# Score halves, then the k and q projections, then the k and q transposes: a new order on TensorE in a windowed-attention pipeline

## The reference, cut to what matters

```
for l in range(2):
    h = shift_token(x)                         # second half of the channels from the token before
    q, k, v = split(h @ wqkv[l], 3)            # 8 heads of 64 channels
    q = l2norm(q) * q_scale[l]; k = l2norm(k) * k_scale[l]
    q, k = rotary_xpos(q, k)                   # a*cos*scale + rotate_half(a)*sin*scale
    o = local_attention(q, k, v)               # windows of 128: own window and the one before, softmax
    x = x + o @ wo[l]
    h = layernorm(shift_token(x)) * ln_g + ln_b
    a, g = split(h @ w1[l] + b1[l], 2)
    x = x + (a * gelu(g)) @ w2[l] + b2[l]
```

## Time and profile before

| | |
|---|---|
| three timed runs | 3395.86, 3398.49, 3399.98 us, median 3398.49 |
| the profiled execution, own time | 3400.02 us |
| its span | 3398.2 us, mean granted TensorE clock 0.956 |
| busy in the span | PE 91%, weight loads 85%, VectorE 74%, ScalarE 70%, GpSimd 54% |
| chain that ended last | PE 77%, VectorE 13%, issue 6% |
| stage 1 | until about 655 us |
| stage 2, steps 4 to 12 (pipeline fills) | 690 to 850 us |
| layer 0 | to about 1978 us; a pair of an even and an odd step takes 42.57 us |
| layer 1 | to about 3290 us; a pair takes 40.92 us |

### The profile page before, as it was taken

The page is one execution under the profiler, slowest core; times in us unless marked ns, Lnnn a source line. Parts: engine busy times, 40 slices in busy tenths (PEclk is TensorE's granted clock), DMA queues, the critical chain, the costliest instruction groups (busy, mean ns, idle before and its releaser), DMA issues.

```text
span 3398.2 us, 68852 instructions
## 1 busy us (share of the span) xinstructions
PE 3089.9 (91%) x22436; PEld 2901.1 (85%) x22436; DVE 2507.5 (74%) x7244; ACT 2394.6 (70%) x5499; POOL 1848.1 (54%) x1761
## 2 busy tenths in 40 slices
PE   7776664179999999999999999999999999999998
PEld 6665553168999999999999989999999999999998
DVE  5999999768777777777777757666667666676664
ACT  4756566457777777777777767777777777777774
POOL 3666666545555555555555545555555555555543
PEclk9988887589999999999999999999999999999999
DMA  2131100155444444444444445544444444444441
GB/s 82 39 136 42 51 27 19 50 117 129 110 109 111 106 111 113 105 107 111 107 111 110 101 125 119 154 110 104 103 103 107 113 111 106 106 106 111 111 102 32
DMA packets 262521, 333.65 MB, mean 98 GB/s; under 512 B 40978, under 2 KB 159508, under 8 KB 261140
## 3 DMA queue, kind: packets, MB, share of 16 engines
q1 hardware_dynamic: 262164, 329.25, 39.4%
HBM read 77.33 MB, written 42.05 MB: 35 GB/s over the span
## 4 chain that ended last, share of the span: by engine, by line
PE 77%; DVE 13%; issue 6%; SPq 1%; DMA 1%; ACT 1%; POOL 1%; DVEq 0%; POOLq 0%; ACTq 0%
PE ps L408 42%; PE ps L490 12%; PE ps L476 6%; PE ps L464 4%; PE ps L465 4%; PE ps L451 3%; DVE aS L891 2%; PE ps L385 2%; PE ps L499 2%; DVE num L899 1%; DVE q L906 1%; DVE BS L927 1%; DVE mS L940 1%; DVE f L916 1%; SPq L1555 1%
## 5 line engine op out<-in xcount | busy, mean ns | idle before, releaser
L751 ACT ACTIVATE Sm<-Sm,nb,sc 128x256 f32<-128x256 f32 (+1 forms) x1024 | 597.6, 588 | 0.8
L1100 DVE CUSTOM_DVE_ANT_0 Sm<-ps,mask 128x256 f32<-128x256 f32 (+1 forms) x1024 | 369.2, 417 | 170.6 <-PE ps L465 168.6
L490 PE MATMUL ps<-vv,PT 128*128 128x64 f32 x4032 | 478.4, 272 | 0.0
L490 PEld LDWEIGHTS ps<-vv,PT 128*128 128x128 f32 x4032 | 470.4, 192 | 0.0
L1173 DVE SCALAR_TENSOR_TENSOR Gl<-ps,vecs,Gl 128x256 f32<-128x256 f32 (+1 forms) x384 | 173.4, 479 | 329.6 <-PE ps L408 284.4
L408 PE MATMUL ps<-zTh,W1h 128*128 128x256 f32 (+1 forms) x1408 | 409.2, 291 | 0.0
L729 ACT ACTIVATE sq<-ps 128x512 f32<-128x512 f32 x256 | 153.2, 599 | 348.2 <-PE ps L408 348.2
L408 PE MATMUL ps<-zTl,W1h 128*128 128x256 f32 (+1 forms) x1408 | 397.2, 282 | 0.0
L408 PE MATMUL ps<-zTh,W1l 128*128 128x256 f32 (+1 forms) x1408 | 391.7, 278 | 0.0
L1380 POOL TENSOR_TENSOR uTl<-Gl,uTh 128x512 fp32r<-128x512 f32 (+1 forms) x192 | 212.9, 1109 | 321.5 <-ACT uTh L800 185.0
L1246 POOL TENSOR_TENSOR rs<-rs,mhalf 128x16 f32<-128x16 f32 x128 | 372.5, 2910 | 0.0
(11 more groups left out here) (189 smaller groups left out, 9538.1 us busy)
## 6 DMA issues: line engine op xcount, KB each, us to landing
kkh<-kh SPq DMA_DIRECT2D x512, 128.0 KB, 2.4
kkl<-kl SPq DMA_DIRECT2D x512, 128.0 KB, 2.4
qq<-qTh SPq DMA_DIRECT2D x256, 128.0 KB, 2.4
qq<-qTl SPq DMA_DIRECT2D x256, 128.0 KB, 2.4
tb<-tab SPq DMA_DIRECT2D x128, 128.0 KB, 2.5
xc<-x SPq DMA_DIRECT2D x32, 256.0 KB, 2.9
rwkv_scratch<-rw SPq DMA_DIRECT2D x32, 256.0 KB, 2.1
rk<-rwkv_scratch SPq DMA_DIRECT2D x64, 128.0 KB, 2.5
```

Source lines behind the costliest of these rows:

```text
L490: ins = pe.matmul(PS[:, k, 64 * i:64 * i + 64], PT[:, h, s * 128:(s + 1) * 128], vv[:, v, h, :], start=s == sides[0], stop=s == sides[-1])
L751: act.activation(Sm[:, h, c0:c1_], Sm[:, h, c0:c1_], ACT.Exp, bias=nb[:, h:h + 1], scale=sc[:, n % 4, h:h + 1], accum_out=sm[:, n % 2, h:h ...
L1100: dve.tensor_tensor_reduce(Sm[:, h, c0:c1_], PS[:, bank["scores", n, q, h % 2], (h // 2 % 2) * 256 + c0:(h // 2 % 2) * 256 + c1_], mask[:, ...
```

## The change

The order inside a step changes in two places that must agree: the list of PSUM users, and TensorE's loop. No instruction is added or removed, and no other engine's program is edited. Waits and increments stay the same, except for the waits on read-outs, which follow from the ring.

```diff
@@ psum_order2
     if live(4):
         yield "scores", t - 4, 0, 0
         yield "scores", t - 4, 0, 1
+        yield "scores", t - 4, 1, 0
+        yield "scores", t - 4, 1, 1
     if live(2):
         yield "qkv", t - 2, 1
-    if live(4):
-        yield "scores", t - 4, 1, 0
-        yield "scores", t - 4, 1, 1
+        yield "qkv", t - 2, 0
     if live(3):
         yield "qkT", t - 3, 1
-    if live(2):
-        yield "qkv", t - 2, 0
-    if live(3):
         yield "qkT", t - 3, 0
     if live(2):
         yield "qkv", t - 2, 2
@@ tensor_program, the loop over t
                 if live(4):
                     scores(t - 4, 0)
+                    scores(t - 4, 1)
                 if live(2):
                     qkv(t - 2, 1)
-                if live(4):
-                    scores(t - 4, 1)
+                    qkv(t - 2, 0)
                 if live(3):
                     turn_qk(t - 3, 1)
-                if live(2):
-                    qkv(t - 2, 0)
-                if live(3):
                     turn_qk(t - 3, 0)
                 if live(2):
                     qkv(t - 2, 2)
```

## The result

The changed kernel takes 3420.22 us (median of 4 runs, 3418.15 to 3421.36), the kernel before 3398.93 on the same chip: a ratio of 1.0063, 95% interval 1.0046 to 1.0081. It is slower by 21 us, on the side that was forecast, but by nearly twice the 11.7 of the sum, and above the range of 3401 to 3417.

The account below looks back on a forecast made before the run. TensorE's own time was taken to bound the kernel, with x2_out on VectorE also pacing layer 0. Terms +6.5 + 3.0 + 3.1 - 0.9 + 0 = +11.7 gave 3411.7, as median 3410; range 3401 to 3417 us.

Parts of the forecast that it names:

- the sum: All terms added for the whole kernel: +11.7 us against the profiled execution's 3400.0, so 3411.7.
- Direction: Whole kernel: slower by over 0.2%, above 3405.3 us, chance 0.72.
- the three waits: ScalarE's queue in layer 0, VectorE's wait in the fill, a bank wait in layer 1: +6.5, +3.0, +3.1 us.
- (c): Pipeline fill: VectorE's rotation of k waits for the later transposes of k, 0.38 late in eight steps, +3.0 us.
- (d): Layer 1, behind odd steps: turn_z waits for its bank until the later q rotation ends, 0.10 a pair, +3.1 us.
- (a): TensorE, eight transposes in a row: saves between nothing and 10 us, taken as 0.
- (b): Odd steps of layer 0: ScalarE's late square of k delays v_out through x2_out, W2 waits 0.25 longer, +6.5 us.
- (e): Border of the layers: 0.95 us of scores now run before the wait for WQ's reload, -0.9 us.
- Rival 4: Slower by more: second bank wait in layer 1's even steps, upper ends of (b) and (c); +19, 3417, chance 0.11.
- Rivals 1 and 2: No measurable change, 3402, chance 0.20; or faster, one return from transposes to products less, 3390.5, chance 0.06.
- Rival 3: TensorE: grouped transposes drop the clock, the v part runs at 1.2 GHz, +164 us, 3574, chance 0.01.

Follow-up runs that it names:

- act_first: Changed kernel with ScalarE's last high part of u and pre_norm moved ahead of the square of k: 3406.67 us, ratio 1.0023.
- two_ak: Changed kernel with two buffers for the rotated k, so its rotation waits for older transposes: 3412.82 us, ratio 1.0046.
- other_bank: Changed kernel with only the bank list reordered, transposes of k ahead of the q part, TensorE's order untouched: 3413.28 us, ratio 1.0038.
- two_ak_act_bank: Changed kernel with the edits of act_first, other_bank and two_ak together: 3392.18 us, ratio 0.9979.
- half_act: half_scores plus the ScalarE edit of act_first: 3389.04 us, ratio 0.9971 against the kernel before.
- half_scores: Kernel before with only scores 1 moved ahead of the k part, transposes left in place: 3405.99 us, ratio 1.0019.
- group_turns: Kernel before with only the q part moved ahead of the transposes of k, scores still split: 3410.00 us, ratio 1.0028.
- tail_late: Changed kernel with VectorE's subtraction of the tail of u moved from ahead of k's rotation to behind the sums: 3429.66 us, ratio 1.0089.

## Why the prediction was wrong, point by point

- **Direction, and the three waits**: right. All three waits that were named are in the profile after, and each goes when its cause is taken away (act_first, two_ak, other_bank). What was missing is under (c) and (d).
- **(a) grouping the transposes, 0**: right within its bounds; two_ak_act_bank against half_act measures a gain of 1.6 us. In layer 0 the eight transposes start at 1164.55 and the v part's first two products at 1165.34 and 1165.65: 0.31 between these, as said, and 1.10 - 0.23 = 0.87 for the eight.
- **(b) ScalarE's queue, +6.5**: right: +5.6 in layer 0 by the table, 0.22 per pair over 25 pairs (0.24 by the medians). half_scores has it alone, act_first takes it away.
- **(c) VectorE's wait in the fill, +3.0**: right in kind, too small in size: +5.1, and just above the upper bound of 5. The distance of 0.81 was exact, but two_ak shows that without the wait the fill would have been 2.5 us shorter than before: the wait costs 7.6. half_scores, with 2.0 less in the fill, points to the earlier scores for the gain. So the 3.0 owes part of its nearness to luck: it left out a gain and a larger cost that stand against each other. Why each step loses as much as it does was not traced further.
- **(d) the ring in layer 1, +3.1: this is the step that failed.** 28 pairs lost 10.6 us, 0.38 a pair (0.36 by the medians) instead of 0.10. The 0.10 of the late rotation is there (group_turns). The distance of turn_z behind the read-out was taken from W2, which starts 0.05 behind; turn_z starts 0.15 behind: another 0.10 a pair. And "VectorE works through from there" left out what stands ahead of the rotation in its queue: ScalarE's delay of (b) was followed to v_out in layer 0 and not to u_hi's other reader, the subtraction of the tail. It meets GpSimd's low part, takes 0.32 longer, and so the rotation of k is 0.25 late instead of 0.10 (20.69 us behind the first product with WO, 20.44 before). That is worth 0.17 a pair by half_scores, the same by other_bank against act_bank (41.07 and 40.90), and 0.15 by act_first against the changed kernel (41.13 and 41.28).
- **(e) the border, -0.9**: the reload's wait fell from 6.08 to 5.71, not to 5.2; the stretch as a whole is at +0.2. So 1.1 us of what the sum lacked are here, little more than two executions differ by.
- **Rival 4** (slower by more, 3417) was nearest, by another way: no second ring wait in even steps. **Rivals 1 and 2** fell with the measured sizes. **Rival 3**, a slower clock: the granted clock is 1.00 in both layers with eight transposes in a row in each of 126 steps. The rule of the Trainium skill cited there (TensorE: Matmul & The Clock Gate, Part 4: PE-mode transpose), that transposes do not count as activity, changes nothing in this kernel: eight transposes in 0.88 us between products leave the clock where it was. Whether transposes count was not tested beyond that.

## What to carry to other kernels

When a block on one engine is moved, follow the instruction that it delays in every other queue to all of its readers, in every kind of step, and look what those readers will run beside: here the delay of one square was priced in layer 0 and cost nearly as much again in layer 1 through a 42-row subtraction. An order that loses may only be badly supplied: the same order on TensorE went from 3420 to 3392 us by three edits, on ScalarE's queue, the banks and the buffers. But ask of each half what it brings: the best kernel here, 3389 us, takes only the first. Before an instruction is moved forward in its queue, list what its semaphores wait for, down to copies of one column, and where these stand in their own queue.

## What the runs showed of the hardware

A VectorE subtraction with both inputs in SBUF (42 x 256) is held while GpSimd reads SBUF, and the trace shows it as a longer instruction, not as idle time: 0.42 us alone, 0.74 to 0.75 beside the low part of u, 0.90 beside the multiplication of the tables. In every case in the changed kernel, half_scores and tail_late (over 180) it ends 0.28 us behind GpSimd's recorded end (2189.83 against 2189.55, 2181.19 against 2180.91, 2200.02 against 2199.75), wherever it started. VectorE's instructions with an input in PSUM don't lengthen: the rotation of q at 2192.33 takes 0.68 while GpSimd works from 2191.29 to 2192.58. The Trainium skill (SBUF — State Buffer, Who interferes with whom) says that a VectorE instruction with two SBUF inputs contends with a GpSimd instruction that reads SBUF, that the shared ports are an exclusive lock, and that the order of issue decides who blocks; the trace agrees: GpSimd starts first, by 0.26 and 0.10 us, and VectorE is held, for the 0.32 us above and for 0.48.

The collision could have been read from the trace of the kernel before. There the last operation of `masked_max` (L1107, 128 x 4, both inputs in SBUF) takes 0.16 us in most steps of layer 0, and 0.35 to 0.70 in 26 of 107, each time beside a GpSimd instruction that reads SBUF and started first, 24 times the low part of nT:

```profile
1135.51 0.74 POOL L1386 TENSOR_TENSOR nTl<-nF,nTh 128x256 fp32r<-128x256 f32 x1 [1.96 <-ACT nTh L712]
1135.84 0.43 DVE L1107 SCALAR_TENSOR_TENSOR nb<-mx,sc 128x4 f32<-128x4 f32 x1
```

It ends 0.02 behind GpSimd's end (1136.27 against 1136.25). Both held instructions end where they would if they had started 0.14 us ahead of that end (0.42 - 0.28 and 0.16 - 0.02), which gives an estimate of what such a meeting costs.

A TensorE block that waits for a semaphore resumes at two distances: in the earlier trace rows the first product of the second W2 block starts 0.05 us behind the read-out, and so does its weight load; turn_z's weight load starts 0.11 to 0.12 behind and its product 0.15. The shorter distance doesn't come from weights that had been loaded ahead:

```profile
1170.67 0.19 PEld L408 LDWEIGHTS ps<-W2h,uTh 128*128 128x128 f32 x1
```

Why the two blocks differ stays open. In tail_late, where the first W2 block of the pair waits for the tail of u, the product starts 0.10 behind. A distance taken from one wait need not hold for another.
